# A language-model block on one core: four engine queues in another order, and the low parts and two block sums on VectorE instead of GpSimd

## What is computed

```python
tok_emb = token_W[sequence] * (sequence != 0)[..., None]
h = tok_emb + pos_emb
attn = softmax(einsum('bnc,bmc->bnm', q, k) + rel_bias) * scale
out = layernorm(einsum('bnm,bmc->bnc', attn, v) @ proj_w + proj_b)
h = h + out
topk_vals, topk_idx = top_k(x_flat @ Wg + bg + bias, 2)
hid = relu(einsum('td,edh->teh', x_flat, W1) + b1)
y = einsum('teh,ehd->ted', hid, W2) + b2
h = h + einsum('ted,te->td', y, combine)
```

## Time and profile before

| | |
|---|---|
| median of 3 runs | 126.74 us (126.0 to 129.31) |
| profiled execution, device time | 126.71 us |
| span of its profile | 124.9 us |
| TensorE busy | 93.4 us (75%) |
| VectorE busy | 75.6 us (61%) |
| ScalarE busy | 67.9 us (54%) |
| GpSimd busy | 61.8 us (49%) |
| DMA | 3.41 MB, mean 27 GB/s |

### The profile page before, as it was taken

The page is one execution under the profiler, slowest core; times in us unless marked ns, Lnnn a source line. Parts: engine busy times, 40 slices in busy tenths (PEclk is TensorE's granted clock), DMA queues, the critical chain, the costliest instruction groups (busy, mean ns, idle before and its releaser), DMA issues.

```text
span 124.9 us, 2801 instructions
## 1 busy us (share of the span) xinstructions
PE 93.4 (75%) x1001; PEld 52.5 (42%) x1001; DVE 75.6 (61%) x319; ACT 67.9 (54%) x134; POOL 61.8 (49%) x120
## 2 busy tenths in 40 slices
PE   0659998537999599969786997608997892995920
PEld 0315955312843365537333652205543360652710
DVE  6789789989940076999599629168241503720462
ACT  1697954313424769864848689107469884427000
POOL 3065069778584004360971565724458170681580
PEclk9999999965556999999999999995599999999995
DMA  1990000000000000000000000010000100004301
GB/s 34 260 387 20 0 0 0 5 0 0 3 0 4 5 0 0 3 0 5 0 0 5 0 0 5 0 42 0 0 0 9 41 0 0 5 0 110 105 0 42
DMA packets 5917, 3.41 MB, mean 27 GB/s; under 512 B 4911, under 2 KB 5264, under 8 KB 5904
## 3 DMA queue, kind: packets, MB, share of 16 engines
q1 hardware_dynamic: 5394, 2.93, 8.0%
q10 hardware_dynamic: 510, 0.31, 1.1%
HBM read 2.17 MB, written 1.06 MB: 26 GB/s over the span
## 4 chain that ended last, share of the span: by engine, by line
PE 32%; DVE 30%; ACT 12%; POOL 12%; issue 8%; DMA 3%; ACTq 1%; DVEq 0%; POOLq 0%
PE bank L1234 5%; PE bank L1261 4%; ACT hid_lo L654 4%; POOL half L522 4%; PE bank L1064 3%; DVE prod L941 3%; POOL rs L496 3%; DMA qkv_sb<-in_qkv_dram 3%; DVE pT L860 3%; PE bank L1258 2%; PE bank L1243 2%; ACT hid_hi L647 2%; POOL half L523 2%; PE bank L1084 2%; PE bank L1270 2%
## 5 line engine op out<-in xcount | busy, mean ns | idle before, releaser
L647 ACT ACTIVATE hid_hi<-bank,b_down 128x512 f16<-128x512 f32 (+1 forms) x40 | 26.0, 650 | 21.1 <-PE bank L1234 21.0
L654 ACT ACTIVATE hid_lo<-bank,b_col 128x512 f16<-128x512 f32 (+1 forms) x40 | 25.9, 649 | 0.0
L522 POOL TENSOR_TENSOR half<-prod 128x256 f32<-128x256 f32 x17 | 12.3, 726 | 27.3 <-DVE prod L941 23.5
L1243 PE MATMUL bank<-hid_hi,minus_h 128*128 128x512 f16 (+1 forms) x40 | 15.3, 384 | 6.7 <-ACT hid_hi L647 6.4
L941 DVE TENSOR_TENSOR prod<-bank,comb 128x512 f32<-128x512 f32 x18 | 12.2, 689 | 12.2 <-PE bank L1264 10.1
L1234 PE MATMUL bank<-xT,w_hi 128*128 128x512 f16 (+1 forms) x40 | 15.4, 385 | 1.3 <-ACT a_sb L625 0.7
L1234 PE MATMUL bank<-xT,w_lo 128*128 128x512 f16 (+1 forms) x40 | 15.1, 379 | 0.0
L1261 PE MATMUL bank<-w_hi,hid_hi 128*128 128x64 f16 x144 | 11.7, 199 | 0.0
L1261 PE MATMUL bank<-w_lo,hid_hi 128*128 128x64 f16 x144 | 11.6, 198 | 0.0
L1261 PEld LDWEIGHTS bank<-w_hi,hid_hi 128*128 128x128 f16 x144 | 9.5, 101 | 4.5 <-issue 4.5
L1243 PEld LDWEIGHTS bank<-hid_hi,minus_h 128*128 128x128 f16 x40 | 4.1, 102 | 16.0 <-ACT hid_hi L647 13.3
(11 more groups left out here) (243 smaller groups left out, 205.0 us busy)
## 6 DMA issues: line engine op xcount, KB each, us to landing
w_sb<-in_w1g_dram SPq DMA_DIRECT2D x1, 516.0 KB, 4.1
hankel<-in_bias_table_dram SPq DMA_DIRECT2D x1, 512.0 KB, 4.4
ids_all<-ids_scratch SPq DMA_DIRECT2D x1, 512.0 KB, 4.3
out_dram<-looked SPq DMA_DIRECT2D x2, 256.0 KB
out_dram<-fin_all SPq DMA_DIRECT2D x3, 128.0 KB
w_sb<-in_w2b_dram SPq DMA_DIRECT2D x1, 260.0 KB, 4.2
vec<-in_vecs_dram ACTq DMA_DIRECT2D x1, 104.5 KB, 4.1
vec<-in_vecs_dram ACTq DMA_DIRECT2D x1, 96.0 KB, 3.1
```

The lines of the kernel that those rows point to most:

```text
L522: link(pool.tensor_tensor(half[:], prod[:, n % 2, 0:4], prod[:, n % 2, 4:8], ALU.add))
L647: act.activation(hid_hi[:, k % 2, e, 0:m], bank[n % LBANKS][:, 0:m], ACT.Relu, bias=b1_down[:, e:e + 1], scale=KEEP * HSCALE / (XSCALE * X ...
L654: act.activation(hid_lo[:, k % 2, e, 0:m], bank[n % LBANKS][:, 0:m], ACT.Relu, bias=b1_col[:, e:e + 1], scale=HSCALE / (XSCALE * XSCALE)). ...
L1243: mm(bank[n % LBANKS][:, 0:m], minus_h[:], hid_hi[:, k % 2, e, 0:m], start=False, stop=True, skip_group_check=True).then_inc(s_rest, 1)
```

## The change

No operation is added to the work or left out of it. Two kinds of operation change engine: `part_low(1)`, `(2)` and `(3)` go from GpSimd to VectorE (`part_low(0)` was there already), and so do `gather(13)` and `gather(15)`, with the final add of unit 3, which belongs to block 13. On VectorE a sum over experts is one reduction instead of three adds. All four lists are written in another order, and three waits are added.

```diff
             def skip_values():
+                pool.wait_ge(s_vh, 1)
                 link(parts(vh_skip[:], lambda i: vs_part[:, i], vs_rest[:]))
...
             def gather(n):
                 u, i = unit_of(n)
                 dve.wait_ge(s_prod, n + 1)
+                if n:
+                    dve.wait_ge(s_gather, n)
                 ins = dve.tensor_reduce(acc[:, i, :], prod[:, n % 2].rearrange("p e d -> p d e"), AX.X, ALU.add)
...
             def skip_scores():
                 pe_.wait_ge(s_egs, 1)
                 pe_.wait_ge(s_skrow, 1)
+                pe_.wait_ge(s_h2, 2)
...
-            table_values(); value_parts(); rsqrt1(0); skip_values(); rsqrt2(0); rsqrt1(1); skip_mix(); rsqrt2(1)
-            part_low(1); bias_parts(); w2_parts(); rsqrt1(2); part_low(2); rsqrt2(2); part_low(3)
-            gather(0); rsqrt1(3); gather(1); rsqrt2(3); gather(2); gather(3); rsqrt1(4); gather(4); gather(5)
+            bias_parts(); w2_parts(); table_values(); skip_values(); value_parts(); rsqrt1(0); rsqrt2(0); rsqrt1(1)
+            rsqrt2(1); skip_mix(); rsqrt1(2); rsqrt2(2); rsqrt1(3); rsqrt2(3); gather(0); gather(1); gather(2)
+            rsqrt1(4); gather(3); gather(4); rsqrt2(4); gather(5); gather(6); gather(7); gather(8); gather(9)
...
-            read_hidden_rows(); centre_bias(); read_qk(); count_late(0); count_late(1); read_v(); table_exps(1)
-            w1_high(); pair_exps(); read_turned_exps(); score_tile(0); squares(0); part_high(0); squares(1)
+            read_qk(); table_exps(1); count_late(0); read_v(); count_late(1); w1_high(); centre_bias(); pair_exps()
+            read_turned_exps(); score_tile(0); squares(0); part_high(0); squares(1); score_tile(1); score_tile(2)
...
-            choose_b(4); weigh(11); weigh(12); read_look(0); weigh(13); read_look(1); read_look(2); weigh(14)
-            weigh(15); weigh(16); weigh(17); gather(17)
+            weigh(8); weigh(9); weigh(10); choose_a(4); weigh(11); choose_b(4); early_one_hots(); weigh(12); weigh(13)
+            gather(13); weigh(14); read_look(0); weigh(15); gather(15); weigh(16); read_look(1); weigh(17)
+            read_look(2); gather(17)
...
-            first_layer(4, 4); look_up(0); first_layer(4, 5); second_layer(13); look_up(1); first_layer(4, 6); look_up(2)
-            first_layer(4, 7); take_high(EXPERTS * UNITS - 1); second_layer(14); second_layer(15); second_layer(16)
-            second_layer(17)
+            second_layer(12); first_layer(4, 6); first_layer(4, 7); second_layer(13); take_high(EXPERTS * UNITS - 1)
+            look_up(0); second_layer(14); second_layer(15); second_layer(16); look_up(1); second_layer(17); look_up(2)
```

70 lines of the change are left out of this document (35 added, 35 removed).

## The result

| | before | changed |
|---|---|---|
| median of 4 runs each, same chip | 126.79 us (126.0 to 129.31) | 109.3 us (109.2 to 109.81) |
| ratio to before | 1 | 0.865, 95% interval 0.860 to 0.870 |
| span of the profile | 124.9 us | 107.4 us |
| end of `embed(1)` | 25.3 | 28.0 |
| last first-layer pass of unit 1 | 60.9 | 55.9 |

The kernel is faster by 13.5%; 107.8 us was forecast. On a second chip the same kernel took 105.44 us, three runs of four at 105.28 to 105.53 and one at 109.41: there TensorE's granted clock averaged 0.971 in the traced run, against 0.928, because it stayed up where it fell on the first chip. Some executions of any of these kernels show a lower granted clock and take some per cent longer than the others, so that a median of four depends on how many of them are in it, and the lowest times are given beside it.

What follows compares the result with a forecast made beforehand. No engine alone was taken to bound the kernel; TensorE's waits from queue order, its lower clock and the look-up did. Terms 26.3 + 29.5 + 36.4 + 13.8 gave 106.0 us of span, 107.8 us of time, range 103 to 115.

Steps and rivals of the forecast that it cites:

- The start: From the beginning to the end of embed(1), 25.3 us before: forecast 26.3 us, between 25.8 and 27.3.
- +0.7 for `centre_bias`, +0.3 for `skip_values`: Before embed(1) ends: centre_bias behind w1_high delays values by 0.7 us; skip_values ahead of value_parts on GpSimd adds 0.3.
- its upper end: Up to the end of embed(1): 27.3 us, if more GpSimd operations are slowed beside VectorE's big weight split.
- the rival made of it: Block sums: VectorE's added two-input SBUF operations slow GpSimd, 12 blocks lose 0.4 us each, 114 us in all; chance 0.05.
- The second stretch: From embed(1) to unit 1's last first-layer pass: forecast 29.5 us, 27.0 to 32.5, with 1.3 us of waits.
- The third stretch: From unit 1's to unit 4's last first-layer pass: 35.0 us of passes plus 1.4 of waits, 36.4, range 35.0 to 38.5.
- The queue order alone made it wait, and cost 4.7 + 2.95 = 7.7 us: Unit 3's choice, choose_a(3), stood behind rows_c(4) on VectorE without needing unit 4; TensorE's wait and lower clock cost 7.7 us.
- The end: After unit 4's last first-layer pass, now with second_layer(13) and all look-ups: forecast 13.8 us, 13.0 to 15.0.
- save GpSimd 1.7 each and cost 1.02: Last stretch: moving two block sums to VectorE saves GpSimd 1.7 us each and costs 1.02.
- The signs: Traces should show values near 17.0, last fin_all at 103.6, and no TensorE wait over 2 us between 28 and 95.
- long stall: Somewhere in 36 to 92 us a queue starves TensorE over 4 us and its clock drops: 115.5 us, chance 0.10.
- "no change" rival: Whole kernel: the new order only moves the stalls and they come back elsewhere, 125.5 us; chance 0.03.

Runs made afterwards that it cites:

- the first experiment: Kernel before with only choose_a(3) moved on VectorE, from behind rows_c(4) to behind rows_b(4): 129.39 us against 126.78 for the kernel before.
- the second experiment: Kernel before with choose_a(3) ahead of rows_c(4), rows_b2(4) ahead of weigh(4), rsqrt2(4) ahead of gather(4) and gather(5): 123.59 us against 130.95.

## Why the prediction was right, point by point

| stretch | forecast | measured | off by |
|---|---|---|---|
| start, to the end of `embed(1)` | 26.3 (25.8 to 27.3) | 28.0 | +1.7 |
| to the last pass of unit 1 | 29.5 (27.0 to 32.5) | 27.9 | -1.6 |
| to the last pass of unit 4 | 36.4 (35.0 to 38.5) | 35.3 | -1.1 |
| the end | 13.8 (13.0 to 15.0) | 16.15 | +2.35 |
| span | 106.0 | 107.4 | +1.4 |

The sum was good because its errors cancel; two of its four terms lay outside their own bounds, and on the second chip the same kernel took 105.4 us. That the total came within 1.5 us was in part luck.

**The start: under-sized.** The term "+0.7 for `centre_bias`, +0.3 for `skip_values`" named the wrong causes. `pbc` was done at 16.94, but values came at 18.12, for VectorE itself was late; GpSimd's early splits, which the prediction put "in time in which it idled" at no cost, stretched `absent_d` from 0.48 to 1.46 us. It was idle time of GpSimd, but not of what it shares with VectorE. Of the 1.8 us by which values came late, 0.7 went with GpSimd's old start and 0.6 more with the old order of VectorE and ScalarE; the remaining 0.5 is little more than the 0.4 us by which two traces of the unedited kernel differ (18.12 and 18.49). In the first trace the value parts added to the loss: `vs_rest` took 1.97 us ahead of them, their last cast took 0.72 us beside VectorE's `p_lo`, `attend(2, 4)` waited 1.65 us for it, and `rsqrt1(0)` came at 25.59. In the second trace `vs_rest` took as long, but the cast ran ahead of `p_lo` in 0.29 us, and `attend(2, 4)` waited 1.44 us for `p_lo` instead. The prediction had given such meetings as the reason for its upper end, and stopped short of what they cost. The Trainium skill ("GPSIMD Engine Reference", "Key points") speaks for the same reading: it says that the two engines contend where VectorE runs an operation of two SBUF inputs or in a two-port mode. The trace agrees for `w_lo`, which reads two tiles of SBUF; `absent_d` reads one, and whether it ran in a two-port mode the trace does not show. It also shows that VectorE loses by a meeting (0.48 to 1.46 us). The prediction had counted one slow operation in the kernel before; there `vh` was another, 1.28 us for two operations that take 0.62 in the changed kernel. The rule also bears on the rival made of it, which was priced for the block sums. Those were not slowed: their first add took 0.73 us on the mean in both kernels. The loss was at the start.

**The second stretch: right, with the clock over-sized.** 9 us at the lower clock were assumed, and it was 6.5 in the first trace (27 to 33.5) and none in the second; TensorE worked in it without a pause, as assumed. Waits of 1.3 us were allowed, and TensorE idled 0.24 (busy 27.66 of 27.9 us); that is 1.06 of the 1.6 us by which the term was too long. How the gain of 7.7 us here divides between TensorE's new order behind `embed(1)`, the shorter stretch of low clock and `skip_turn`, for which VectorE had waited 8.22 us before and now waits 0.85, no run has taken apart. The moved `part_low` had been costed as free on VectorE and as a help to GpSimd's square roots: the help is about 0.5 us.

**The third stretch: right.** Its count, 12 pairs at 1.77 us and 12 passes at 1.15, is 35.0, and 35.3 was measured with 0.3 instead of 1.4 us of small waits. In VectorE's timeline of the changed kernel, the choice of unit 3 and the norm of unit 4:

```profile
70.74 0.18 DVE L910 SCALAR_TENSOR_TENSOR lg<-bank,gb_sum 128x32 f32<-128x32 f32 x1
...
75.42 0.62 DVE L726 TENSOR_TENSOR xn<-xc,rs 128x256 f32<-128x256 f32 x1
```

and GpSimd's, the square root of that norm, ahead of the sum of block 5:

```profile
73.94 1.12 POOL L501 TENSOR_TENSOR rs<-var,neghalf 128x4 f32<-128x4 f32 x1 [1.03 <-DVE var L720]
75.04 0.72 POOL L523 TENSOR_TENSOR half<-prod 128x256 f32<-128x256 f32 x1
```

The choice is made at 70.74, 12.5 us sooner than before (5.0 of them were there at the end of unit 1), and the square root ends 0.36 us ahead of `xn`. But the reason was only half right. The prediction's step "The queue order alone made it wait, and cost 4.7 + 2.95 = 7.7 us" fell, as far as it meant that one call, in the first experiment: moved by itself, the call brought 1 us of span. The price was nearly right, 6.1 us for 7.7, and the second experiment shows where the other half lay, in `rsqrt2(4)` behind two block sums. The prediction had seen that row and asked of `turn(4)` only whether it was in time in the new order.

**The end: under-sized by 2.35 us.** TensorE's rows there:

```profile
92.49 0.86 PE L1274 MATMUL bank<-fin_part,oneh_t 128*128 128x64 bf16 x24
...
96.76 0.37 PE L1262 MATMUL bank<-b_k,ones_b 3*128 3x512 bf16 x1 [1.02 <-DVE prod L941]
```

`look_up(0)` waits for nothing, as forecast. The sum left out three things. `gather(13)` waited 1.24 us for GpSimd's sum of block 12, itself behind 2.1 us of `early_one_hots` on VectorE that the change had put there. `gather(15)` waited 0.64 more. And TensorE, at work for only 10.8 of 16.15 us, lost its clock at 98.7: `look_up(1)` and the block behind it took from 97.78 to 102.84, 5.1 us instead of the 3.8 of the sum. The last `fin_all` came at 104.61 instead of 103.6. The credit for two sums on VectorE ("save GpSimd 1.7 each and cost 1.02") came to 0.2 us at most.

**The signs.** Of those that the prediction named as right, two failed: `values` came at 18.12 instead of about 17.0, and the last `fin_all` at 104.61 instead of 103.6. The others held: no wait of TensorE over 2 us, none of `choice_exp(3)`, none of `look_up(0)`, 1.77 us from one second layer to the next over one pass.

**The rivals.** No long stall came up: TensorE's longest wait from 28 to 95 us is 0.69. But the "no change" rival, that waits only move, describes what single parts of this change do: the two parts done alone in the kernel before, the choice and the look-ups, brought 1 us or less. Each met another queue position that held up the same stretch, GpSimd's `rsqrt2(4)` in the one case and ScalarE's `choice_exp(4)` in the other. It failed for the change as a whole, which moves those too.

**What is left open.** Of the 17.5 us of span the runs tie 6.1 to the two calls of units 3 and 4. The moves to VectorE are worth about 0.5 and 0.2 us, so nearly all of the gain is order, but which of the other moved calls bring how much was not tested.

## What to carry to other kernels

Follow a stall back until nothing in the chain waits for a queue's order, and price the repair of all its causes together; here the first cause removed alone brought 1 us, and put back in the finished order it cost 4.8. Treat VectorE and GpSimd as one resource when filling idle time of either with wide SBUF work beside a critical chain of small operations. Check a good forecast term by term: here two terms that were too small and two that were too large made it look better than its reasoning.

## What the runs showed of the hardware

An operation of VectorE and one of GpSimd that meet can stop each other for as long as the other's whole instruction: `absent_d` 1.46 us for 0.48 beside a split on GpSimd, and `vs_rest` 1.97 us (0.29 before) and `vh_rest` 2.04 (0.44 for an operation of the same size a microsecond sooner) beside `w_lo` on VectorE and the operation ahead of it. Three meetings show this; which pairs of operations meet so and which don't was not sorted out.

One and the same kernel took 109.3 us on one chip and 105.4 on another, and 2.5 us of the 3.7 between their spans lie in a stretch in which only the first lost its clock; the rest lies in the start (0.4) and in the end (0.8), where both lost it, the first sooner. In the first trace TensorE was busy 0.99 of 3 us from 24 to 27 and was given 1.2 GHz until 33.5; in the second it was busy 1.56 of 3 and kept 2.4 GHz. That does not part the two cases: the variant with the low parts back was busy 1.69 of the same 3 us, and its clock fell all the same (0.56 from 26 to 27, 0.50 from 28 to 34). From `embed(1)` to block 13 the first took 63.3 us and the second 60.75. Why it fell early in a variant with the old start was not settled.
